# The shared bias is added to x on GpSimd instead of VectorE, in seven of eight sequences

## What is computed

```
xn = layernorm(x)
g, v, d = xn @ Wg + bg, xn @ Wv + bv, xn @ Wd + bd
scan: h[s] = a[s] * h[s-1] + sigmoid(g) * tanh(v),  a = 0.001 + 0.998 * sigmoid(d)
scores = sigmoid(xn @ Wg_e.T + bg_e + bias); the two best of 8 experts
expert(e) = gelu(xn @ W1[e].T + b1[e]) @ W2[e].T + b2[e]
shared = gelu(xn @ Ws1.T + bs1) @ Ws2.T + bs2
out = x + scan + shared + sum over the two best of score * expert
```

## Time and profile before

| | |
|---|---|
| median of 3 runs | 710.67 us |
| the profiled execution | 710.67 us, span 708.8 us |
| busy: PE, DVE, ACT, POOL | 94%, 72%, 61%, 40% |
| chain that ended last | PE 75%, DVE 13%, issue 5%, ACT 3% |
| L828 (the add on DVE) | 8 of 1216 ns, from 36.4 us to 253.4 us |
| L896 in the first part | 64 of 480 ns (median) |
| L897 in the first part | 64 of 752 ns (mean) |

### The profile page before, as it was taken

One profiled execution on the slowest core, in us unless ns is written; L12 is line 12 of the kernel. 1 busy time (PEld: TensorE's weight loads), 2 busy tenths in 40 slices (PEclk: granted clock), 3 DMA queues, 4 the chain that ended last, 5 costly groups with the idle time before them and its releaser, 6 DMA issues.

```text
span 708.8 us, 20193 instructions
## 1 busy us (share of the span) xinstructions
PE 665.5 (94%) x5872; PEld 521.3 (74%) x5873; DVE 513.5 (72%) x1329; ACT 430.4 (61%) x738; POOL 285.4 (40%) x261
## 2 busy tenths in 40 slices
PE   4879999999999999699999999999999999999993
PEld 3455747565656565488988888888888888898773
DVE  5878989898989888766667666676666666666652
ACT  7967776868686855455555555555555555555651
POOL 2132332323242424234554645545446455463421
PEclk9999999999999999999999999999999999999997
DMA  7424334342516131222433323334333243332421
GB/s 258 169 71 139 90 120 112 97 137 71 172 57 182 35 120 31 70 44 60 67 52 61 67 53 66 57 60 66 55 60 66 53 67 54 61 65 50 72 40 23
DMA packets 54172, 57.55 MB, mean 81 GB/s; under 512 B 13204, under 2 KB 48916, under 8 KB 54136
## 3 DMA queue, kind: packets, MB, share of 16 engines
q1 hardware_dynamic: 38456, 38.42, 18.4%
q0 software_dynamic: 15680, 18.69, 16.4%
HBM read 38.53 MB, written 18.55 MB: 81 GB/s over the span
## 4 chain that ended last, share of the span: by engine, by line
PE 75%; DVE 13%; issue 5%; ACT 3%; DMA 2%; POOL 0%; DVEq 0%; SPq 0%; ACTq 0%; POOLq 0%
PE bank L1213 33%; PE bank L1205 29%; PE bank L1232 3%; PE bank L1193 3%; PE bank L1262 2%; PE bank L1244 2%; DVE W L800 2%; DVE arena L896 1%; DVE arena L839 1%; DVE arena L897 1%; PE bank L1184 1%; DVE arena L852 1%; DVE small L809 1%; DMA arena<-in_gates 1%; PE bank L1149 1%
## 5 line engine op out<-in xcount | busy, mean ns | idle before, releaser
L1213 PE MATMUL bank<-W,arena 128*128 (+1 forms) x2304 | 305.8, 274 | 16.0 <-DVE arena L897 14.0
L1205 PE MATMUL bank<-rows,W 128*128 128x256 f16 (+1 forms) x1920 | 299.2, 294 | 0.3 <-issue 0.2
L1213 PEld LDWEIGHTS bank<-W,arena 128*128 128x128 f16 x2304 | 222.4, 98 | 58.0 <-DVE arena L897 20.4
L1205 PEld LDWEIGHTS bank<-rows,W 128*128 (+1 forms) x1920 | 186.2, 98 | 54.5 <-issue 0.8
L592 ACT ACTIVATE arena<-bank,par 128x256 f32<-128x256 f32 x256 | 134.0, 559 | 80.3 <-PE bank L1205 69.3
L502 POOL DMA_INDIRECT out<-arena,slot_add x64 | 109.7, 1714 | 146.4 <-ACT arena L729 136.6
L896 DVE TENSOR_SCALAR arena<-arena,par 128x256 f16<-128x256 f32 x284 | 101.7, 358 | 81.7 <-ACT arena L592 54.8
L897 DVE SCALAR_TENSOR_TENSOR arena<-arena,par 128x256 f16<-128x256 f32 x284 | 138.7, 488 | 10.1
L438 POOL DMA_INDIRECT lists<-entry,place x64 | 67.9, 1061 | 150.6 <-ACT arena L578 73.2
L487 POOL DMA_INDIRECT rows<-xhl_rows,slot_list x64 | 68.9, 1076 | 51.8 <-DMA slot_list<-lists 34.8
L600 ACT ACTIVATE rows<-bank 128x1024 f16<-128x1024 f16 x32 | 32.7, 1023 | 60.9 <-PE bank L1262 33.4
(11 more groups left out here) (157 smaller groups left out, 519.9 us busy)
## 6 DMA issues: line engine op xcount, KB each, us to landing
stage<-in_w SPq DMA_DIRECT2D x32, 512.0 KB
b2row<-in_b SPq DMA_DIRECT2D x39, 128.0 KB
arena<-in_x SPq DMA_DIRECT2D x8, 512.0 KB
xhl_rows<-W SPq DMA_DIRECT2D x8, 512.0 KB
out<-arena SPq DMA_DIRECT2D x8, 512.0 KB
W<-in_w SPq DMA_DIRECT2D x4, 512.0 KB, 9.3
lists<-entry,place POOLq DMA_INDIRECT x64
rows<-xhl_rows,slot_list POOLq DMA_INDIRECT x64
```

Source lines behind the costliest of these rows:

```text
L1205: ins = T.matmul(bank_, weights(w, wp * HALF + c * H + j * P, P), rhs[:, 2 * xp + c, :], start=n == 0, stop=n == 3 * KD - 1)
L1213: ins = T.matmul(banks[t // 2][:, (t % 2) * D:(t % 2 + 1) * D], h[:, hp, t * P:(t + 1) * P], weights(w, (2 + wp) * HALF + j * D, D), start ...
```

## The change

In sequences 1 to 7 the add is no longer issued by VectorE at the end of the sequence before. GpSimd issues it instead, in its own program, after the fourth scatter of the sequence before. It waits for `xs_ok` as the old one did, and a new semaphore, `base_ok`, tells VectorE's `residual` that x has its bias. Sequence 0 is as before.

```
-PER = 45
+PER = 44
+        dec_ok, base_ok = sem("dec_ok"), sem("base_ok")
...
@@ gpsimd
+            def add_bias(b, u):
+                v = chunks(xt[u], TPB)
+                pool.wait_ge(xs_ok, b + 1)
+                if b == 1:
+                    pool.wait_ge(bs2_in, 16)
+                pool.tensor_tensor(out=v, in0=v, in1=bs2[:, :].unsqueeze(1).to_broadcast([P, TPB, D]),
+                                   op=ALU.add).then_inc(base_ok, 1)
...
                 for c in range(4 if b + 1 < SEQS else 8):
                     scatter(b, c)
+                if b + 1 < SEQS:
+                    add_bias(b + 1, (b + 1) % 2)
...
@@ vector, residual
+                if i == 0 and not (isinstance(b, int) and b == 0):
+                    dve.wait_ge(base_ok, b)
...
@@ vector, end of opening
                 split_wide(0, 7)
-                add_bias(1, 1)
...
@@ vector, end of sequence
                 else:
-                    add_bias(b + 1, 1 - u)
                     low_part(b + 1, 0, 1)
```

More of the change, by code:

```diff
@@ L253, in layer @@
         hhl_ok, y_ps, y_ok = sem("hhl_ok"), sem("y_ps"), sem("y_ok")
-        dec_ok = sem("dec_ok")
+        dec_ok, base_ok = sem("dec_ok"), sem("base_ok")
         scan_ok, scanT_ps, r_ok = sem("scan_ok"), sem("scanT_ps"), sem("r_ok")
```

## The result

The changed kernel takes 719.59 us (median of 4 runs, 718.31 to 720.15) beside 710.94 for the one before on the same chip: ratio 1.0121, 95% interval 1.0103 to 1.0138. It is slower by 8.7 us, where 2.1 were forecast. A second series gave 718.53 beside 710.97, ratio 1.0105 (1.0088 to 1.0122).

A forecast was written before the change was run, and what follows sets the result against it. The prediction took TensorE as the bound, with a few waits on VectorE's tail. Sequence 0 +1.8, sequence 6 +0.9 and five steady boundaries -0.55 gave +2.15 on 710.67: 712.8 us, range 705.0 to 716.0.

The forecast's parts named there:

- Part 1, the gain of 5.4 us: Seven adds leave VectorE; five steady boundaries gain 0.96 to 1.13 us each, about 5.4 us; the other two gain 0.
- Part 2, the new wait costs nothing: VectorE's `residual` also waits for GpSimd, but the add has over 20 us of lead: cost 0.
- Part 3, an add of 2.2 us: Length of GpSimd's add, estimated from its fills: 2.2 us, with ends at 1.74 and 2.54 us.
- Part 4, the two engines exclude each other: GpSimd's add and VectorE's two-tensor or fast one-input instructions lock each other out of SBUF; sum +2.15 us, chance 0.57.
- Rival 1: No blocking, or only in slivers, between GpSimd and VectorE: the gain alone remains, 705.3 us; chance 0.20.
- Part 4, steady sequences: Add runs after split 5's second instruction; split 6 is 1.58 us late, net gain 0.1 each, -0.55 for five.
- Part 4, sequence 0: Add follows L800, both last splits 2.29 us late, 0.48 to spare: TensorE loses 1.8 us on the path.
- Part 4, sequence 6: Add follows the earlier fourth scatter, split 1.91 us late, 1.01 to spare: TensorE loses 0.9 us on the path.
- Rival 2: GpSimd's add is longer than its streams, 3.2 us as by a software loop: 719.7 us; chance 0.08.
- Rival 3: Blocking, but idle gaps or turns mean about half of each overlap is paid: -1.6 us, 709.1 us; chance 0.15.

The follow-up runs named there:

- experiment 1: Changed kernel without the seven adds, GpSimd only signals and the waits stay: 705.65 us beside 711.10 for the kernel before, ratio 0.9923.
- experiment 3: Changed kernel, but GpSimd's add also waits for the end of split 5: 714.47 us beside 711.10 for the kernel before, ratio 1.0053.
- experiment 4: Changed kernel with the add ahead of the fourth scatter, released by ScalarE's last high part: 710.81 us beside 711.43 for the kernel before, ratio 0.9989.
- experiment 5: Changed kernel, add still behind the scatter but also waiting for ScalarE's last high part: 710.71 us beside 710.97 for the kernel before, ratio 0.9997.
- experiment 8: Changed kernel with a one-input GpSimd copy into a free tile instead of the add: 709.75 us beside 711.43 for the kernel before, ratio 0.9973.
- experiment 9: Changed kernel with two GpSimd fills into a free tile instead of the add: 706.35 us beside 711.43 for the kernel before, ratio 0.9924.
- second profile: The changed kernel run again unchanged, profiled for its start: 718.53 us beside 710.97 for the kernel before, ratio 1.0105.
- first profile: Profile from the changed kernel's first series: 719.59 us beside 710.94 for the kernel before, ratio 1.0121.
- experiment 10: Against the kernel before, adds of sequences 2 to 6 on GpSimd behind their own sequence's power and multiply: 707.91 us beside 711.10, ratio 0.9953.

## Why the prediction was wrong

The sign was right, the size not: 712.8 forecast, 719.6 measured, beyond the upper end of 716.0. The step that failed is the beginning of the add in part 4's steady sequences.

- **Part 1, the gain of 5.4 us.** Right: 5.5 us by experiment 1. The chain of the earlier trace rows was the limit at five boundaries, and the two others gave nothing. The last boundary gave 1.11 us too, more than its 0.96 of idle time, which no row explains.
- **Part 2, the new wait costs nothing.** Right, by the same experiment, which keeps the wait.
- **Part 3, an add of 2.2 us.** 2.35, a mis-sizing of 0.15, or 1 us in the sum.
- **Part 4, the two engines exclude each other.** Right, and it decides the sign. Rival 1 falls: experiments 3, 4, 5, 8 and 9 all show VectorE held.
- **Part 4, steady sequences: the step that failed.** "VectorE's L897 at 114.90 + 0.75 = 115.65; the add then has SBUF to 117.85." I let the add queue behind the split's running second instruction and hold the next split by 1.6 us, net -0.55 for five. In the changed kernel the add already had SBUF when that instruction asked for it, so it was held itself, by 2.60 us, and TensorE waited 1.64 us for it; the idle time of 0.62 us before split 6, which was to absorb part of the delay, absorbed none of it: +4.5 us for five. The start of a GpSimd row is not the moment from which it holds SBUF; behind the indirect DMA that moment lay 0.45 to 0.96 us earlier. This one step is 5 of the 6.8 us missing. Experiment 3 confirms it: with the add begun behind the running instruction, as I had it, the five come out at -0.48.
- **Part 4, sequence 0: +1.8.** Right, 1.7 in the second profile; there the low part (L800, L811 after the change) had started first and the add waited for it, as I had it. The other 1.7 of the first profile goes with the longer half clock, for which the sum had no term although the trace before has a half clock there too. It is the other part of the missing 6.8.
- **Part 4, sequence 6: +0.9.** 1.2 measured, near enough for an add 0.15 us longer. The add's beginning was right, since the instruction ahead reads one SBUF tensor (L858, with a PSUM one) and was not held.
- **Rival 2** gave 719.7, by an add of 3.2 us. The number is hit by luck; the add takes 2.35.
- **Rival 3**, half of the overlaps paid, falls: an instruction that meets the add is held until the add ends.

## What to carry to other kernels

Moving an elementwise instruction from VectorE to GpSimd paid here only where no VectorE instruction on the path that reads two SBUF tensors or is of the fast one-input form had to run meanwhile. Where GpSimd's instruction reads SBUF, as the add and the copy here do, count the whole of it as a stall of each such place, and don't count from its recorded start: behind an indirect DMA, with its waits already over, it shut VectorE out within 0.54 us of the DMA's start. Put it where the trace shows VectorE waiting for another engine for as long as it lasts (experiment 10). If it must stand in a tight place, give it a wait that ends just after the start of the VectorE instruction which has to go first (experiment 5). Here place and one wait made 707.9, 710.7 and 719.6 us, with the same result computed.

## What was not expected of the hardware

- A GpSimd add of 128 x 1024 fp32 takes 2.35 us, a copy 1.04, a fill 0.95; the same add on VectorE 1.22.
- The add shuts VectorE out before its row begins when an indirect DMA (0.96 us) is being executed ahead of it: a two-tensor VectorE instruction that started 0.45 us before the add's row was held for 2.60 us; with the add's wait ending 0.22 us after that instruction's start it was not held (0.75 us).
- No running VectorE instruction was seen to be interrupted: the add's own row got longer instead, by 0.17, 0.32 and 0.5 us in experiments 5, 4 and 10.
- A held instruction ends 0.56 us (two inputs, 512 elements) or 0.28 us (fast form) after GpSimd's. That is about the time which its elements alone take: 256 more of them cost 268 ns in L910 and 132 ns in L909 (480 ns less 348).
- A fill held the fast one-input form (1.30 instead of 0.48 us), not the two-tensor form.
- An instruction that reads one tensor of SBUF and one of PSUM (L858) took 0.68 us beside the add, as everywhere.
- TensorE's half clock after a pause of 3.65 us lasted until about 52 us in one execution of the changed kernel and about 58 us in another; sequence 0 was 1.7 us longer in the second of these.
